# Attention scores as two fp32r parts in two row halves of TensorE, the output turned by block transposes, and the expert tables in three steps

## The chip, the cores and the metric

The kernel runs on one core of one Trainium2 chip. The metric is the device time of one execution in microseconds (us). TensorE is called PE here (its weight loads PEld), VectorE DVE, ScalarE ACT, GpSimd POOL and SyncE SP.

## The reference, cut to what matters

The input is x of 8 batches by 512 tokens by 256 features. After a layer norm come two attention mixers with layer norms between them, and then a mixture of 8 experts of which each token takes 2.

```python
# token mixer: 16 heads of 16 features, the same projection for queries and keys
dot = einsum('bhnd,bhmd->bhnm', qk, qk);  q2 = sum(qk * qk, -1)
logits = (2 * dot - q2[..., :, None] - q2[..., None, :]) / sqrt(dh) * tau
out = einsum('bhnm,bhmd->bhnd', softmax(logits), v) -> (b, n, 256) @ Wo
# channel mixer: 8 heads of 32 channels over the 512 tokens, the same form
# experts: softmax router, top 2, gelu(x @ w1 + b1) @ w2 + b2, weighted sum
x = x + layernorm(attention(layernorm(x)));  x = x + layernorm(ffn(layernorm(x)))
```

All of it is float32. Where the kernel before wants more than bf16 or fp32r gives, it splits a number into parts and multiplies the parts.

## The kernel before, in words

**Order of the work.** Each engine has its own program, and all five are made from one schedule by hand. A batch b is a body of 16 positions (`schedule`, L87). At each position comes the attention of batch b (`att`), then the steps that tables name for that position: POST_AT for batch b-1 (what follows its attention), LATE_AT for b-2 (router), EARLY_AT for b+2 (first norm) and PRE_AT for b+1 (its projections), and then `att_end`. Batches 0 and 1 fill the pipeline, 2 to 5 run in a loop, and 6 and 7 drain it. After batch 7 come the experts: 16 units of 512 rows and 7 of 256, one after the other. What is left of batches 6 and 7 is put between their groups by slots (TAIL_AT, L77); a unit of 512 rows has 16 slots, 8 in its first product and 8 in its second.

**Scores.** At a position PE makes the scores of two units (one head each, 256 keys by 512 queries), four matmuls of 512 columns, into two buffers of PS (L974). ACT turns each unit into E with one exponential of 1024 elements (L589). PE may write the scores of unit u when the exponential of unit u-2 has ended. The operands OPA and OPB hold 102 rows: q in three bf16 parts, paired so that one product gives six terms, and the norms in three parts with ones against them. DVE makes the parts (L696 to L700 for q, L713 to L719 for the norms), SP stores them in memory and loads them in their pairing (L325 to L335 and L371, L377), 11 transfers to a group of four heads. In the first batch ACT's queue loads the keys and norms of the first group.

**The second product.** At `att_end` PE multiplies E by the values (L957): four heads side by side in four column groups of 32, float32 in two passes, eight instructions to a position. ACT copies the sums to OT once in four positions (L597).

**After the attention.** `untok` turns OT with 16 PE transposes (L1036) into PSUM, DVE divides by the sum of the weights (L730, L732) into ON, `ontok` turns ON back with 8 PE transposes (L1047) and ACT copies them to OTN (L549), and `proj` multiplies by Wo (L1058). Then follow the channel mixer's steps: z2, x2t, qkc (L1058), gram (L1093), dist (L1102), soft_c, weights_c, mix (L1111), weff (L1120) and, a body later, chan (L1058 again) with `chan_add`. POOL makes the residual that the projection is added to. The positions 0, 5 and 9 carry chan, proj and qkc, 16 instructions each; at position 12 PE has no step.

**Tables.** DVE works out which rows each expert unit takes. `fill_begun` (L1229), 20 dependent operations, does it for the 5 units that batches 0 to 5 fix; it comes at position 9 of the last body. `fill_tables` (L1281), 51 dependent operations, does the rest at slot 52, and until it ends POOL holds the gather of unit 5. From unit 5 on the second product of the experts is in the joined form (L1767, L1768), before that in the plain one (L1772).

**Start.** SP issues the transfers of x, the vectors, the constants and the weights, with the last four weights in one transfer (L361), and PE's first scores wait for the norms of the first group.

## Time and profile before

| | |
|---|---|
| median of 3 runs | 1119.0 us (1118.0 to 1121.36) |
| the profiled execution's own time | 1118.23 us |
| span of its trace | 1116.4 us |
| mean granted PE clock | 0.975 of 2.4 GHz |
| PE, PEld, DVE, ACT, POOL busy | 92%, 63%, 60%, 65%, 34% |
| first scores; bodies 0, 1, 2 to 5, 6, 7 start at | 32.0; 32.0, 76.4, 136.2, 401.5, 468.0 us |
| last expert unit ends, last output | about 1060 us, 1116 us |

The bodies' starts are the first scores (L974) of position 0 in PE's timeline. A loop body takes 265.3 / 4 = 66.3 us. A busy share is an average over stages; the windows of the trace give it stage by stage.

### The profile page before, as it was taken

Reading aid. Unit: us, or ns where it says so; the run is one execution under the profiler, and the core shown is the slowest. Engines: PE = TensorE matmul, PEld = TensorE weight load, DVE = VectorE, ACT = ScalarE, POOL = GpSimd, SP = SyncE. Lnnn points to the kernel's source line nnn. Section 1 sums busy time; section 2 is a strip of 40 time slices with the busy share of each in tenths; the row PEclk is TensorE's granted clock in tenths of the full one; section 3 lists DMA queues with packets and bytes.
Section 4 is the critical chain, followed back from the end, with each engine's and each line's share of the span. In section 5 each row is a group of like instructions: output and inputs, shape, how many; then the busy total and the mean of one; then the engine's idle time right before and its main releaser. Section 6 shows DMA issues by size and latency. Waiting matters only on the chain. (4 is left out here: it accounts for less than half of the span.)

```text
span 1116.4 us, 17406 instructions
## 1 busy us (share of the span) xinstructions
PE 1032.4 (92%) x5756; PEld 702.8 (63%) x5756; DVE 671.4 (60%) x1902; ACT 721.1 (65%) x1106; POOL 384.5 (34%) x353
## 2 busy tenths in 40 slices
PE   5899999999999999998899996999999999989966
PEld 3234545555455455544588875888888888878842
DVE  5225265454735645354785777677677776679927
ACT  2797767667776766666655662676677766768804
POOL 5121030513323141224426243444433443254315
PEclk9899999999999999999999987999999999989989
DMA  7673816427082542832433133334443344446456
GB/s 267 133 246 61 264 31 204 122 84 256 18 261 73 174 150 69 275 148 91 147 100 115 62 135 123 124 133 148 147 161 119 138 143 142 151 143 224 149 215 256
DMA packets 48960, 167.47 MB, mean 150 GB/s; under 512 B 10160, under 2 KB 16688, under 8 KB 42864
## 3 DMA queue, kind: packets, MB, share of 16 engines
q1 hardware_dynamic: 38170, 136.94, 36.9%
q0 software_dynamic: 10560, 29.14, 8.2%
q8 instruction: 40, 0.66, 0.3%
q10 hardware_dynamic: 150, 0.41, 0.2%
q14 instruction: 40, 0.33, 0.1%
HBM read 102.74 MB, written 63.70 MB: 149 GB/s over the span
## 5 line engine op out<-in xcount | busy, mean ns | idle before, releaser
L589 ACT ACTIVATE E<-PS,VV 128x1024 f32<-128x1024 f32 x256 | 271.6, 1119 | 73.7 <-PE PS L974 72.6
L1737 PE MATMUL PH<-XP,W1P 128*128 128x512 f32 (+1 forms) x1104 | 233.1, 369 | 4.9 <-DVE HP L1678 4.5
L1737 PEld LDWEIGHTS PH<-XP,W1P 128*128 128x128 f32 x1104 | 185.8, 192 | 44.5 <-DVE HP L1678 8.1
L974 PE MATMUL PS<-OPB,OPA 102*128 102x512 bf16 x512 | 137.9, 386 | 11.4 <-DMA OPB<-norm_parts 5.7
L1678 DVE TENSOR_TENSOR HP<-PH,HP 128x512 fp32r<-128x512 f32 x156 | 106.7, 686 | 64.8 <-ACT HP L1584 64.3
L957 PE MATMUL PO<-E,VA 128*32 128x512 f32 x1024 | 143.5, 610 | 0.0
L1579 ACT ACTIVATE PH<-PH,B 128x512 f32<-128x512 f32 (+1 forms) x184 | 107.5, 596 | 53.9 <-PE PH L1737 44.9
L1502 POOL DMA_INDIRECT choice_rows<-Y,DI x78 | 79.3, 1016 | 182.3 <-DVE Y L1635 160.8
L974 PEld LDWEIGHTS PS<-OPB,OPA 102*128 102x128 bf16 x512 | 37.7, 98 | 155.4 <-ACT E L589 68.7
L1570 ACT CAST W2P<-WG 128x512 fp32r<-128x512 f32 x92 | 56.9, 621 | 103.6 <-PE PB L1768 63.6
L462 POOL DMA_INDIRECT expert_rows<-PAY,SLOT x64 | 62.7, 979 | 157.5 <-issue 80.1
L1767 PE MATMUL PY<-W2P,HP 128*128 128x512 f32 x288 | 110.6, 412 | 5.0 <-DVE Y L1635 5.0
L1672 DVE TENSOR_TENSOR W2P<-WG,W2P 128x512 fp32r<-128x512 f32 x92 | 82.0, 900 | 43.5 <-ACT W2P L1570 42.6
L1584 ACT CAST HP<-PH 128x512 fp32r<-128x512 f32 x156 | 91.7, 588 | 4.9
L1495 POOL DMA_INDIRECT XG<-expert_rows,RI x78 | 82.4, 1056 | 32.5 <-issue 26.1
L1768 PE MATMUL PY<-W2P,HP 128*128 128x256 f32 x288 | 81.6, 283 | 0.0
L1767 PEld LDWEIGHTS PY<-W2P,HP 128*128 128x128 f32 x288 | 55.2, 192 | 18.2 <-DVE Y L1635 6.6
L1767 PE MATMUL PB<-W2P,HP 128*128 128x512 f32 x176 | 65.6, 395 | 0.0
L1667 DVE TENSOR_TENSOR W1P<-WG,W1P 128x512 fp32r<-128x512 f32 x92 | 59.6, 687 | 8.3 <-ACT W1P L1563 8.3
L1772 PE MATMUL PY<-W2P,HP 128*128 128x256 f32 x480 | 63.6, 292 | 0.0
L1772 PEld LDWEIGHTS PY<-W2P,HP 128*128 128x128 f32 x480 | 60.8, 198 | 0.1
L1058 PE MATMUL PB<-WB,OTN 128*128 128x256 f32 x256 | 58.8, 383 | 0.2 <-issue 0.2
(254 smaller groups left out, 1611.2 us busy)
## 6 DMA issues: line engine op xcount, KB each, us to landing
expert_rows<-ZERO SPq DMA_DIRECT2D x8, 4160.0 KB, 12.8
WG<-experts SPq DMA_DIRECT2D x23, 1152.0 KB, 5.1
WG<-experts SPq DMA_DIRECT2D x23, 1028.0 KB, 5.2
OPB<-q_parts SPq DMA_DIRECT2D x192, 64.0 KB
YC<-choice_rows SPq DMA_DIRECT2D x8, 1024.0 KB, 13.0
q_parts<-QP SPq DMA_DIRECT2D x48, 128.0 KB
OPA<-q_parts SPq DMA_DIRECT2D x31, 192.0 KB
X<-x SPq DMA_DIRECT2D x8, 512.0 KB, 11.1
```

The source lines that it names most:

```text
L589: a.activation(E[:, s % 2, h, :, :], PS[:, u % 2, :, :], ACT.Exp, scale=vec("tau_t")[:, 4 * (s // 2) + h:4 * (s // 2) + h + 1]).then_inc(e ...
L957: i = t.matmul(PO[32 * h:32 * h + 32, :], VA[:, par, 2 * jp + jc, 4 * g + h, :], E[:, s % 2, h, jc, :], start=(jp == 0 and jc == 0), stop= ...
L974: ins = t.matmul(PS[:, u % 2, jc, :], OPA[0:KA, m, key:key + P], OPB[0:KA, m, hh * N:hh * N + N], start=True, stop=True)
L1495: g.indirect_dma_start(out=XG[:, t % 2, i, :], out_offset=None, in_=rows, in_offset=IND(ap=RI[:, b // HALVES, b % HALVES:b % HALVES + 1], ...
L1579: last = a.activation(r, r, ACT.Gelu_apprx_tanh, bias=B1[:, n * j + k:n * j + k + 1])
L1584: a.copy(region(0, j), PH[:, u % BANKS, :]).then_inc(h_hi, 1)
L1672: v.tensor_tensor(second_piece(1, q), second_raw(q), second_piece(0, q).bitcast(f32), ALU.subtract).then_inc(w2_lo, 1)
L1678: v.tensor_tensor(region(1, j), PH[:, u % BANKS, :], region(0, j).bitcast(f32), ALU.subtract).then_inc(h_lo, 1)
L1737: last = m.matmul(PH[:, u % BANKS, at:at + w], W1P[:, a, k * HID + c * P:k * HID + c * P + P], XP[:, o, k, 0:w], start=(k == 0 and (a, o) ...
L1767: m.matmul(sums(i), HP[:, 0, at:at + P], W2P[:, c, :, :], start=(c == 0), stop=(c == HC - 1), skip_group_check=True)
L1768: last = m.matmul(sums(i)[:, 0, :], HP[:, 1, at:at + P], W2P[:, c, 0, :], start=False, stop=(c == HC - 1), skip_group_check=True)
L1772: last = m.matmul(PY[:, i, :], HP[:, a, at:at + P], W2P[:, c, o, :], start=(c == 0 and (a, o) == terms[0] and i % 2 == 0), stop=(c == HC - ...
```

## The change

Scores: q is split into two fp32r parts (a rounded one and the rest), the norms too, so that three terms of 16 rows and four rows of norms and ones make KA = 52 rows. Two heads lie in partitions 0 to 51 and 64 to 115, and their matmuls write different banks. A unit is now two heads by 128 keys, and ACT makes two exponentials of 512 elements for it. Untok: DVE turns 32 by 32 blocks, divides, and turns the blocks back; the rows of Wo are put in the order that this leaves. Tables: `fill_begun` runs twice, for 5 units and for 2 more (at slot 17), and `fill_tables` does the rest at slot 75. SP alone loads the norms, those of the first group included, and Wo is loaded in 8 transfers.

```diff
-BEGUN = -(-(2 * N * (B - 2) - NE * (2 * SUB - 1)) // (2 * SUB))
+KNOWN = [-(-(2 * N * b - NE * (2 * SUB - 1)) // (2 * SUB)) for b in (B - 2, B - 1)]
+BEGUN = KNOWN[-1]
-KA = 102
-PRE_USES, POST_USES, LATE_USES = 7, 18, 4
+KA = 3 * DH + 4
+PRE_USES, POST_USES, LATE_USES = 7, 12, 4
-LOADS = 16 * 11
-PARTS = 16 * 3
+LOADS = 16 * 12
+PARTS = 16 * 2
-POST_AT = {2: ['residual', 'untok0'], 3: ['untok1'], 4: ['ontok'], 5: ['proj'], 6: ['z2'], 8: ['x2t'], 9: ['qkc'], 10: ['gram'],
-           11: ['dist'], 12: ['soft_c'], 13: ['weights_c'], 14: ['mix'], 15: ['weff']}
+POST_AT = {1: ['untok0'], 2: ['residual', 'untok1'], 4: ['proj'], 5: ['z2'], 7: ['x2t'], 8: ['qkc'], 9: ['gram'],
+           10: ['dist'], 11: ['soft_c'], 12: ['weights_c'], 13: ['mix'], 14: ['weff']}
...
-           17: [('prefix', B - 2)], 18: [('x2t', B - 1)], 20: [('qkc', B - 1)], 22: [('gram', B - 1)], 24: [('dist', B - 1)],
...
-           52: [('tables', B - 1)]}
+           17: [('prefix', B - 2), ('begin', B - 2)], 19: [('x2t', B - 1)], 22: [('qkc', B - 1)], 25: [('gram', B - 1)],
...
+           71: [('prefix', B - 1)], 75: [('tables', B - 1)]}
```

The operands and their loads (`load_queries` is like `load_keys`):

```diff
+        OPA = sb("OPA", [P, KC, PAIRED, N], f32r)
+        OPB = sb("OPB", [P, KC, PAIRED, N], f32r)
...
         def load_keys(eng, b, g):
+            for r in range(2):
+                v = q_rows(g, r)
+                eng.dma_start(operand(OPA, g, r, 0, 2 * DH), v).then_inc(op_loaded[g], 16)
+                eng.dma_start(operand(OPA, g, r, 2 * DH, DH), v[0:DH]).then_inc(op_loaded[g], 16)
...
+        def load_norms(eng, b, g):
+            eng.wait_ge(n_stored, 16 * (b + 1))
+            for r in range(2):
+                eng.dma_start(operand(OPA, g, r, 3 * DH, 2), norm_rows(g, r)).then_inc(op_loaded[g], 16)
+                eng.dma_start(operand(OPB, g, r, 3 * DH + 2, 2), norm_rows(g, r)).then_inc(op_loaded[g], 16)
...
-            sp.dma_start(WB[:, :, :, :], wview[:, 2:6]).then_inc(w_rest, 16)
+            sp.dma_start(WB[:, 1:4, :, :], wview[:, 3:6]).then_inc(w_rest, 16)
+            for h in range(H // KC):
+                q, g = h % 4, h // 4
+                at = 32 * q + DH * g
+                sp.dma_start(WB[at:at + DH, 0, :, :], wview[DH * h:DH * h + DH, 2]).then_inc(w_rest, 16)
```

DVE's split and untok, ACT's exponentials, PE's scores:

```diff
-                    pre.did(v.tensor_tensor(QR[:, m, :], QF[:, m, :], QP[:, m, 0, :], ALU.subtract))
-                    pre.wait()
-                    pre.did(v.tensor_copy(QP[:, m, 1, :], QR[:, m, :]))
-                    pre.wait()
-                    v.tensor_tensor(QP[:, m, 2, :], QR[:, m, :], QP[:, m, 1, :], ALU.subtract).then_inc(qp_ready, 1)
+                    v.tensor_tensor(QP[:, m, 1, :], QF[:, m, :], QP[:, m, 0, :].bitcast(f32), ALU.subtract).then_inc(qp_ready, 1)
...
+                    dve.wait_ge(po_read, GROUPS * b + 2 * m + 2)
+                    for r in range(2):
+                        post.did(v.transpose(TK[:, r, :], OT[:, 2 * m + r, :]))
+                    post.wait()
+                    blocks = TK[:, :, :].rearrange("p r (j e) -> p r j e", e=32)
+                    post.did(v.reciprocal(REC[:, :, :], blocks[:, :, :, DH]))
+                    post.wait()
+                    for r in range(2):
+                        post.did(v.tensor_tensor(TN[:, m, :].rearrange("p (j r d) -> p r j d", r=2, d=DH)[:, r], blocks[:, r, :, 0:DH],
+                                                 REC[:, r, :].unsqueeze(2).to_broadcast([P, N // 32, DH]), ALU.mult))
+                    post.wait()
+                    v.transpose(OTN[:, m, :], TN[:, m, :]).then_inc(otn_ready, 1)
...
+                for jc in range(2):
+                    u = 4 * s + 2 * (pos % 2) + jc
                     act.wait_ge(s_full, UNITS * b + u + 1)
+                    for r in range(2):
+                        h = 2 * (pos % 2) + r
+                        ins = a.activation(E[:, s % 2, h, jc, :], PS[:, u % 2, r, :], ACT.Exp,
+                                           scale=vec("tau_t")[:, 4 * (s // 2) + h:4 * (s // 2) + h + 1])
+                    ins.then_inc(e_ready, 1)
...
+                for jc in range(2):
+                    u = 4 * s + 2 * (pos % 2) + jc
                     at_least(pe, e_ready, UNITS * b + u - 1)
+                    key = (2 * (s % 2) + jc) * P
+                    for r in range(2):
+                        at = HALF_ROWS * r
+                        ins = t.matmul(PS[:, u % 2, r, :], OPA[at:at + KA, m, pair, key:key + P], OPB[at:at + KA, m, pair, :],
                                        start=True, stop=True)
                     ins.then_inc(s_full, 1)
```

PE's untok and ontok and ACT's ontok are taken out; the norms' split loses two of its four operations; and the gather of the first unit of the last table (now unit 7) goes to its ordinary place.

## Rows read from the trace of the kernel before

**Rows 1.** The page, part 1: busy time of the engines.
```profile
PE 1032.4 (92%) x5756; PEld 702.8 (63%) x5756; DVE 671.4 (60%) x1902; ACT 721.1 (65%) x1106; POOL 384.5 (34%) x353
```
**Rows 2.** Busy time by stage: loop bodies, body 7, the tail's first units.
```profile
core 0: us, PE busy (x) PEld busy (x) DVE busy (x) ACT busy (x) POOL busy (x), PEclk, DMA share, GB/s
...
136.20:401.50 265.30, 256.51 (x1493) 137.19 (x1490) 140.35 (x528) 185.44 (x236) 74.21 (x70) 1.00 0.44 140
...
468.00:532.40 64.40, 58.68 (x340) 29.46 (x336) 29.65 (x125) 42.34 (x53) 22.61 (x24) 0.95 0.39 135
532.40:714.00 181.60, 160.38 (x972) 140.58 (x969) 131.59 (x373) 100.15 (x170) 76.92 (x70) 0.93 0.34 115
```
**Rows 3.** PE's timeline in a loop body: start us, length us, line, operation.
```profile
302.54 1.04 PE L974 MATMUL PS<-OPB,OPA 102*128 102x512 bf16 x4
303.41 1.04 PE L1077 MATMUL PB<-KT,ON 128*128 128x128 f32 x8
304.28 0.60 PE L1135 MATMUL PA<-KT,PAY 128*128 128x128 f32 x4
304.81 1.07 PE L957 MATMUL PO<-E,VA 128*32 128x512 f32 x8
305.81 1.04 PE L974 MATMUL PS<-OPB,OPA 102*128 102x512 bf16 x4
306.74 3.69 PE L1058 MATMUL PB<-WB,OTN 128*128 128x256 f32 x16
```
**Rows 4.** ACT's timeline in a loop body.
```profile
348.07 0.59 ACT L528 COPY QF<-PA 128x512 f32<-128x512 f32 x1 [1.16 <-PE PA L1005]
348.56 0.59 ACT L529 CAST QP<-PA 128x512 bf16<-128x512 f32 x1
349.40 2.12 ACT L589 ACTIVATE E<-PS,VV 128x1024 f32<-128x1024 f32 x2 [0.26 <-PE PS L974]
```
**Rows 5.** PE's timeline in the experts: fp32r matmuls of 512 columns.
```profile
714.54 11.36 PE L1737 MATMUL PH<-XP,W1P 128*128 128x512 f32 x48
```
**Rows 6.** The page, part 5: weight loads of those matmuls.
```profile
L1737 PEld LDWEIGHTS PH<-XP,W1P 128*128 128x128 f32 x1104 | 185.8, 192 | 44.5 <-DVE HP L1678 8.1
```
**Rows 7.** DVE's timeline in a loop body: untok, and the split of q.
```profile
350.56 0.42 DVE L732 TENSOR_TENSOR ON<-PB,REC 128x256 f32<-128x256 f32 x1
...
354.07 0.68 DVE L696 TENSOR_TENSOR QR<-QF,QP 128x512 f32<-128x512 f32 x1
```
**Rows 8.** PE's timeline at the start: the first scores.
```profile
32.00 1.89 PE L974 MATMUL PS<-OPB,OPA 102*128 102x512 bf16 x4 [5.73 <-DMA OPB<-norm_parts]
```
**Rows 9.** PE's timeline in the tail: idle before an instruction in brackets.
```profile
552.39 1.19 PE L1036 MATMUL PB<-KT,OT 128*128 128x128 f32 x8 [2.70 <-DVE ON L732]
...
678.55 1.11 PE L1748 MATMUL PT<-KT,XG 128*128 128x128 f32 x4 [8.02 <-DVE XP L1661]
679.32 8.19 PE L1772 MATMUL PY<-W2P,HP 128*128 128x256 f32 x48
...
726.10 0.47 PE L1767 MATMUL PY<-W2P,HP 128*128 128x512 f32 x1
...
731.73 0.60 PE L1748 MATMUL PT<-KT,XG 128*128 128x128 f32 x4
```
**Rows 10.** The same timeline: an undisturbed second product in the plain form.
```profile
708.71 6.00 PE L1772 MATMUL PY<-W2P,HP 128*128 128x256 f32 x48
```
**Rows 11.** DVE's timeline: first and last operation of fill_begun (20) and fill_tables (51), and a wait.
```profile
511.56 0.21 DVE L1253 TENSOR_TENSOR QR<-COUNT,KT 128x56 f32<-128x56 f32 x1
...
516.02 0.07 DVE L1276 MEMSET DUMP<- 128x20 f32 x1
...
661.80 0.15 DVE L1305 SCALAR_TENSOR_TENSOR OT<-TAKEN,COUNT 128x8 f32<-128x8 f32 x1
...
675.70 0.17 DVE L1367 CAST WI<-OT 128x7 int32<-128x7 f32 x1
...
688.85 0.16 DVE L1648 TENSOR_TENSOR NT<-XG 128x4 f32<-128x4 f32 x1 [6.04 <-DMA choice_rows<-Y,DI]
```

More of the change, by code:

```diff
@@ L329, in load_queries, with operand @@
[L329 to L335 removed]
+        def operand(tile, g, r, at, n):
+            first = g % 2 * 2
+            return tile[HALF_ROWS * r + at:HALF_ROWS * r + at + n, g // 2, first:first + 2, :].bitcast(f32)
@@ L545, in scalar_program @@
             do["v0"], do["v1"] = vv(0), vv(1)
-            def ontok(b, par):
-                for m in range(KC):
-                    a.copy(OTN[:, m, :], takep(b, 4 + m)).then_inc(post_free[m], 1)
-            do["ontok"] = ontok
             def x2t(b, par):
                 for k in range(KC):
-                    affine(X2T[:, k, :], takep(b, 8 + k), vec("ln2_w")[:, k:k + 1], vec("ln2_b")[:, k:k + 1]
+                    affine(X2T[:, k, :], takep(b, 2 + k), vec("ln2_w")[:, k:k + 1], vec("ln2_b")[:, k:k + 1]
                            ).then_inc(post_free[k], 1)
@@ L1248, in fill_begun @@
     rows_of, most = COUNT[:, 0, :], STEPS_E // 2 - 1
-    over, full, start, ends = take(NE, most), take(NE), take(NE), take(NE)
+    over, full, start, ends, ahead = take(NE, most), take(NE), take(NE), take(NE), take(NE)
     cube, held = take(NE, NE), take(U, NE)
@@ L1258, in fill_begun @@
     link(v.tensor_tensor(ends, start, full, ALU.add))
-    link(v.tensor_scalar(start, start, -1.0, float(U), ALU.mult, ALU.add))
-    link(v.tensor_tensor(start, start, full, ALU.min))
-    link(v.tensor_scalar(TAKEN[:, :], start, 0.0, None, ALU.max))
     unit = const("unit")[:, 0:2 * U].rearrange("p (u two) -> p u two", two=2)[:, :, 0]
@@ L1928, in constants @@
     put("expert_steps", np.diff(v % NE, prepend=0))
-    put("unit", s // 2)
+    put("unit", np.arange(max(LEFT, 2 * BEGUN)) // 2)
     put("offset", s % 2 * SUB)
```

245 lines of the change are left out of this document (109 added, 136 removed).

## The prediction

> **What bounds the kernel now.** I read the busy shares first: PE has 92%, the next engines 65% and 60% [rows 1]. The windows then tell where. In the loop bodies PE is busy 256.5 of 265.3 us at the full 2.4 GHz, ACT 185 and DVE 140 [rows 2]: PE sets the 66.3 us of a body, and what is taken from PE there comes off the time until ACT is next. Body 7 (64.4 us, 58.7 busy) and the tail with the first expert units (181.6 us, 160.4 busy, clock 0.93) have gaps. Each position is a chain too: ACT needs 2.02 us for its two units, 1.01 for each (2.12 is the length of two that overlap a little) [rows 4]. A position cannot be shorter than that, whatever PE saves.
>
> I checked this reading by adding up a body. On PE four scores take 0.87 us, from their start to the next instruction's; the second product takes 1.00; a 128 column instruction takes 0.109 (eight in 0.87), a 256 column one 0.22 (sixteen in some 3.5) [rows 3]. Between the four transposes at 304.28 (0.44) and the second product at 304.81 there are 0.09 more, which I take as the price of changing the form of the array; I use 0.12. A position is the longer of 1.99 + its steps on PE, and 2.02 + its copies on ACT. From 0 to 15 this gives 5.95, 3.2, 4.6, 4.6, 2.9, 5.5, 3.7, 2.5, 3.9, 7.3, 3.75, 2.9, 2.6, 2.5, 4.6, 5.5: 66.0, against 66.3 measured. So the model may carry the change.
>
> **Scores.** 64 bf16 matmuls of 512 columns in a body become 64 of fp32r with 52 rows, in 32 pairs whose halves may run together. No row shows row halves. Bounds: fp32r at 512 columns takes 11.36 / 48 = 0.237 us in the full array, loads included [rows 5]. If the halves run together, two pairs take 0.47; if not, four take 0.95, against 0.87 now. The nearest row is the second product: eight instructions of 512 columns in four column groups take 1.00 us [rows 3], where eight of 0.237 in a row would take 1.9. The array does run groups side by side, and the two halves write different banks, so I take 0.47: 0.40 less at a position. Then scores and steps no longer have the same form: one more change, between nothing and 0.15; I take the 0.12, at the 13 positions with steps.
>
> The Trainium skill, TensorEngine Tiling (Array Packing), Key Properties, says that changing the tiling mode drains TensorE. The 0.09 above agrees; were each drain a full 0.15, a body would be 0.4 us longer than I say.
>
> **Untok and ontok.** 24 transposes leave PE: 24 x 0.109 = 2.6 us in a body, with them two copies on ACT (1.0 us). In their place DVE has six block transposes of 512 elements, two reciprocals and four products. No row shows a block transpose. The nearest are a subtraction of 512 from SBUF, 0.68 long and 0.6 apart, and the division of 256, 0.42 [rows 7]; I take 0.6 for each transpose, at most 1.2 if it runs at half pace. A half of untok then is 1.2 + 0.3 + 0.7 + 0.7 = 2.9 us, 5.8 in a body in place of some 2.6. The split drops two of its three operations on each half of q and two of four on the norms; with 0.4 for a copy to bf16 (an estimate from the 0.42) and 0.7 for a subtraction that is 3.3 us back. DVE stays near 35 of 61 us: covered, if its order holds. At position 1 untok0 now stands before chan_add, so chan_add ends near 12.7 us into the body, the residual on POOL near 16.6, and untok1 near 15.6. PE's proj at position 4 wants it at 16.2. That is 0.6 us of slack; at half pace PE would wait some 2 us.
>
> **ACT.** 64 exponentials of 512 in place of 32 of 1024. Two copies of 512 stand 0.49 apart, two units of 1024 1.01 [rows 4]: two of 512 cost 0.98, so no more. Bound: 0.6 each, were nothing overlapped, 6 us of a body that has 20 us of ACT to spare, felt only where ACT leads.
>
> **The body after.** With 0.47 + 0.12 + 0.12 + 1.00 = 1.71 plus steps, or ACT's sum: 5.7, 3.2, 3.4, 3.4, 5.2, 2.5, 3.4, 3.9, 5.7, 5.3, 2.6, 2.6, 2.1, 3.1, 5.3, 3.5 = 60.9. That is 5.1 us less than the same sum before. PE's own saving is larger, 6.4 in scores less 1.6 in changes plus 2.6 = 7.4; the rest is lost at positions 1, 5, 7, 11, 12 and 13, where ACT leads. The steps after proj keep their distances: I followed proj's last add, norm, z2 and x2t, and gram, dist, soft_c and mix, and found the waits of before (under 1 us each) moved and not grown.
>
> Four loop bodies give 20.5 us, body 6 some 5, bodies 1 and 7, which miss some steps and have ACT ahead more often, 4.5 each. In body 7 fill_begun moves behind gram's copies, so its 4.5 us [rows 11] keep soft_c instead of dist waiting: even. Body 0 is mostly ACT's: 1.5. Together 36.
>
> **Transfers.** q's parts in memory are 8 bytes for 6, the operands as many bytes as before (96 rows of 2 against 48 of 4, twice), 12 issues for 11 on SP. In the loop PE is idle 3% of the time in all and DMA busy 44% [rows 2], so no load is late now, and I add nothing. At the start PE waits 5.73 us for the norms [rows 8]. The two dropped split operations come before that store, and one queue issues four small loads where two queues issued one each; Wo's eight transfers only delay x of later batches by some 3 us. The gain is between 0 and the 5.73; I take 1, since the keys on ACT's queue still start behind the same copy.
>
> **Tail.** Off: the 2.6 us of transposes of batch 7, the idle 2.70 at 552 [rows 9], about 2.5 us of small waits by wider slots, and POOL's held gather, which made DVE wait 6.04 for a send [rows 11] and PE about 1.8. On: the second fill_begun, 26 operations at 4.5 / 20 = 0.23 each, 5.9 us of DVE at slot 17, of which PE's three banks hide a part: 4.5. fill_tables runs 14.0 us and leaves PE idle 8.02, then slow: 8.19 against 6.00 [rows 9, 10, 11]. With 25 subtiles for 29 it takes 13.4; at slot 75 PE has four chunks (6 us) less DVE's lag before it: idle 9.7, 1 us worse. Units 5 and 6 keep the plain form: a half costs 714.54 - 708.71 = 5.83 for the joined one's 731.73 - 726.10 = 5.63, so 0.4 a unit, 0.8 for two [rows 5, 9, 10]. Sum: -9.6 + 6.3 = -3.
>
> **The sum.** -36 - 1 - 3 = -40 against the profiled execution's own 1118.2, thus 1078.2. That execution stands 0.8 us below the median, so for a median **1079 us**. Unknown sizes: pair time 0.47 to 0.6 (+0 to +10), changes of form 0 to 0.15 (-10 to +3), untok at half pace (0 to +13), tail (-6 to +6). Alone this case spans 1066 to 1098.
>
> **Rival 1: the halves do not run together.** For it: no row shows them. Against it: the column groups do. Scores then take 0.95; with the change of form a position costs 0.2 more, 13 x 0.2 = 2.6, which is what the transposes gave. Bodies stay at 66, start and tail give 4: 1115.
>
> **Rival 2, slower: weight loads in the open.** An fp32r load is 192 ns long [rows 6]. Were the halves to run one after the other, with one load exposed before each unit, the scores would take 0.95 + 0.38 = 1.33: +0.46, +0.12 for the change, 13 x 0.58 - 2.6 = +4.9 in a body, 32 over the kernel, less 4: 1147. It is slower as soon as the four scores take over 0.95. Against it: 48 such loads hide behind their matmuls in 11.36 us, no more than 20 ns each showing [rows 5].
>
> The Trainium skill, TensorE: Matmul & The Clock Gate, Part 3, says that a load overlaps running matmuls only if it goes to other row groups. Here each second pair reloads the same halves. The 11.36 us contradicts this in the full array, where all loads use the same rows; in halves no run shows it yet.
>
> **Rival 3: PE becomes faster, but DVE's chain is late.** Block transposes at 1.2, proj late by 2 to 3 us, and everything after it behind: +2.5 x 6 bodies and some in the tail: 1096. For it: only 0.6 us of slack. Against it: SBUF operations of that size take 0.6.
>
> **How the numbers follow.** My case 0.70, rival 3 0.12, rival 1 0.11, rival 2 0.07. A measurement can tell 0.3%, 3.4 us, from no change: rival 1 lies at that border, 0.05 of it within, 0.01 above, 0.05 below. Faster 0.87, same 0.05, slower 0.08. The range of 8 in 10 takes my case nearly whole and rival 3: 1064 to 1100.
>
> **What would show it.** Right: the scores start two and two, the two pairs of a position within about 0.47; loop bodies of 61 us; ACT's exponentials 0.5 apart; PE's idle time put down to ACT at positions 1, 5, 7, 11 to 13; the tables' idle near 10 us in unit 4. Wrong: each score starting 0.2 us after the last (rival 1); gaps before loads (rival 2); PE waiting for OTN at position 4 with DVE's transposes over 1 us (rival 3); or a granted clock below 1.00 in the loop, which I do not expect, with PE over 90% busy.

## The result, and the profile after

The changed kernel took 1135.05 us (median of 4 runs, 1130.59 to 1135.85), the kernel before, beside it on the same chip, 1118.5. The ratio is 1.0129, 95% interval 1.0097 to 1.0161: **slower by some 14 us**, where I had forecast 1079. The profiled execution took 1130.59 us (span 1128.8), that of the kernel before 1118.23 (span 1116.4): 12.4 us between them.

The table cuts both traces at the same marks: the first scores, ACT's copies of OT (the first of each body), the first expert product, PE's transposes ahead of unit 5's second product, the first product of the last unit, and PE's first instruction of stage 3. The marks do not fall on the borders of bodies, so a forecast stands beside the stretch that lies nearest.

```
stretch                                before    after   difference   forecast
to the first scores                     32.0      31.95     0.0         -1
first scores to first OT copy           18.0      20.5     +2.5         -1.5 (body 0)
to OT of body 2                        113.0     111.7     -1.3         -4.5 (body 1)
to OT of body 6 (four bodies)          265.2     259.6     -5.6        -20.5
to OT of body 7                         67.2      68.2     +1.0         -5
to the first expert product             42.7      44.6     +1.9         -4.5 (body 7)
to unit 5's second product (tail)      187.7     193.7     +6.0         -3
to the last unit's first product       327.0     327.3     +0.3          0
to stage 3's first PE instruction       20.4      27.9     +7.5          0
to the end                              43.2      43.4     +0.2          0
```
By the first scores of each body, body 0 takes 48.2 us for 44.4, body 1 57.6 for 59.8, a loop body 65.0 for 66.3, body 6 64.5 for 66.5, and body 7, up to the first expert product, 74.2 for 70.1. Between the forecast of -40 and the +12.4 of the traces lie 52 us: 34.5 in the bodies, 9 in the tail, 7.5 in the gap before stage 3 and 1 at the start. (The last expert unit of the kernel before ends at 1065.1 us, not at about 1060 as its table says.)

The page of the changed kernel: busy time of the engines, ACT's exponentials, PE's scores.
```profile
PE 999.9 (89%) x5628; PEld 685.7 (61%) x5628; DVE 685.9 (61%) x1904; ACT 745.6 (66%) x1346; POOL 385.8 (34%) x353
...
L607 ACT ACTIVATE E<-PS,VV 128x512 f32<-128x512 f32 x512 | 310.8, 716 | 67.9 <-PE PS L993 67.3
...
L993 PE MATMUL PS<-OPB,OPA 52*128 52x512 f32 x512 | 108.3, 474 | 33.1 <-ACT E L607 26.2
```
PE works 32 us less than before [rows 1], and the kernel is longer. ACT works 25 us more: the exponentials bring 39 (310.8 here, 271.6 on the page of before), and ontok's 16 copies are gone.

Busy time by stage: four loop bodies, body 7, and the tail with its first units.
```profile
core 0: us, PE busy (x) PEld busy (x) DVE busy (x) ACT busy (x) POOL busy (x), PEclk, DMA share, GB/s
137.67:397.83 260.16, 238.07 (x1396) 125.15 (x1393) 149.47 (x520) 198.24 (x356) 75.05 (x70) 1.00 0.52 148
462.32:531.50 69.18, 55.37 (x317) 28.58 (x313) 34.80 (x130) 46.27 (x84) 23.52 (x24) 0.90 0.41 135
531.50:714.50 183.00, 155.57 (x948) 134.12 (x948) 137.12 (x390) 98.50 (x168) 74.63 (x68) 0.95 0.33 112
```
Against [rows 2]: a loop body is 65.0 us for 66.3. PE's work in it fell by 4.6 us (256.5 to 238.1 over four), its idle time rose from 2.2 to 5.5. So 3.3 of the 4.6 us that left PE came back as waiting.

PE's timeline in a loop body, positions with scores, the wait at proj, and scores that ACT holds up.
```profile
307.07 0.73 PE L993 MATMUL PS<-OPB,OPA 52*128 52x512 f32 x4
307.73 2.05 PE L1090 MATMUL PB<-ON 128*128 128x128 f32 x16
...
317.01 0.50 PE L993 MATMUL PS<-OPB,OPA 52*128 52x512 f32 x2
318.17 0.49 PE L993 MATMUL PS<-OPB,OPA 52*128 52x512 f32 x2 [0.66 <-ACT E L607]
...
351.78 3.72 PE L1056 MATMUL PB<-WB,OTN 128*128 128x256 f32 x16 [2.12 <-DVE OTN L750]
```
Four scores take 0.66 us to the next instruction where nothing waits, for 0.87 in [rows 3]. My sum had 0.59 for this: 0.47, and 0.12 for the change of form behind the scores. Taken apart, the operations on PS of one position (ns: shortest, median, longest):
```profile
L993 PEld LDWEIGHTS PS<-OPB,OPA x4: 182/184/186, 301.2 to 301.3; 52*128 52x128 f32 x4
```
```profile
L993 PE MATMUL PS<-OPB,OPA x4: 393/444/496, 301.2 to 301.5; 52*128 52x512 f32 x4
```
The four matmuls start within 0.34 us and are each 0.39 to 0.50 long: the halves do run together. The 0.19 by which the step is longer than 0.47 is the length of one of its loads. That the first load of a position lies in the open is my reading; no run here isolates it. The Trainium skill, TensorE: Matmul & The Clock Gate, Part 3, has loads overlap running matmuls only for other row groups. The trace does not agree for the second pair: its two loads start at 301.27 and end at 301.46, while the matmuls of the first pair, in the same halves, are recorded from 301.17 to 301.66. At the first load of a step the numbers allow the rule.

ACT's timeline in the loop body: four exponentials are 2.47 us long for the 2.12 of two long ones [rows 4].
```profile
302.24 2.47 ACT L607 ACTIVATE E<-PS,VV 128x512 f32<-128x512 f32 x4
```
Back to back they stand 0.57 apart, so two of 512 cost 1.14, where one of 1024 cost 1.01. Body 0, which is mostly ACT's, grew by 3.8 us (e2 below, the scores alone, has the same 48.2).

DVE's timeline in a loop body: both halves of untok (block transposes, then the two products), chan_add between them; then POOL's residual.
```profile
340.14 1.31 DVE L741 STREAM_TRANSPOSE Z3T<-OT 128x512 f32<-128x512 f32 x2
...
341.87 0.76 DVE L747 TENSOR_TENSOR ON<-Z3T,REC 128x256 f32<-128x256 f32 x2
...
344.79 1.23 DVE L842 TENSOR_TENSOR X<-X 128x1024 f32 x1 [0.16 <-DVE X L840]
345.94 1.30 DVE L741 STREAM_TRANSPOSE Z3T<-OT 128x512 f32<-128x512 f32 x2
...
347.65 3.24 DVE L747 TENSOR_TENSOR ON<-Z3T,REC 128x256 f32<-128x256 f32 x2
350.93 0.71 DVE L750 STREAM_TRANSPOSE OTN<-ON 128x512 f32<-128x512 f32 x1
```
```profile
346.69 1.90 POOL L472 TENSOR_TENSOR X<-X,SM 128x1024 f32<-128x1024 f32 x1 [0.19 <-POOL SM L470]
348.67 1.95 POOL L475 TENSOR_TENSOR X<-X,SM 128x1024 f32<-128x1024 f32 x1
```
A block transpose takes 0.65, near the 0.6 I had taken. But the same two products take 0.76 in the first half and 3.24 in the second, where POOL's residual runs from 346.7 to 350.6. Taken apart, the first product takes 1.21 us and ends 0.28 after POOL's first operation, the second takes 2.11 and ends 0.28 after POOL's second. The surplus of 2.5 us covers the 2.12 for which PE waits at proj.

The kernel before holds the control. POOL's residual ran beside untok's products there too, and did not slow them:
```profile
349.20 1.89 POOL L453 TENSOR_TENSOR X<-X,SM 128x1024 f32<-128x1024 f32 x1
```
The product at 350.56 in [rows 7] lies inside this operation and took 0.42. It read one operand from PSUM; the new products read both from SBUF. None of the products of L732 that meet the residual in that trace is longer than 0.43, and the new block transpose that meets it (the second at 345.94) takes 0.67.

At the start nothing moved: 31.95 for the 32.00 of [rows 8]. The tail, PE: idle before an instruction in brackets (compare [rows 9]).
```profile
555.57 2.93 PE L1745 MATMUL PH<-XP,W1P 128*128 128x512 f32 x6 [3.74 <-DVE HP L1686]
...
594.72 1.65 PE L1745 MATMUL PH<-XP,W1P 128*128 128x512 f32 x3 [5.85 <-DVE HP L1686]
...
716.46 13.95 PE L1745 MATMUL PH<-XP,W1P 128*128 128x512 f32 x48 [10.47 <-DVE XP L1669]
730.25 0.60 PE L1756 MATMUL PT<-KT,XG 128*128 128x128 f32 x4
```
The second fill_begun runs on DVE from 588.35 to 593.84 (26 operations, 5.5 us), and holds HP. The 48 products behind the tables' wait take 13.95 where undisturbed ones take 11.36 [rows 5]: the granted clock is 0.50 from 708.3 us on, for 13.7 us.

The end of the experts' block: POOL's last instruction there (ns), and PE's first of stage 3.
```profile
L1161 POOLq DRAIN  x1: 9221/9221/9221, 1075.9 to 1075.9; - x1
```
```profile
1085.45 4.82 PE L1853 MATMUL S<-KT 128*128 128x128 f32 x21 [15.58 <-PEq L1161]
```
In the kernel before, this drain took 1707 ns and PE was idle for 8.08 us. Nothing in the program touches that place.

### The profile page after: what moved, and what is told of

Its sections match the earlier page's. It is cut to its first block and busy times, and to the rows that moved or that the text cites. A ratio compares the mean times of both kernels' runs of the same rounds, so it can differ in the third digit from the quotient of the medians.

```text
span 1128.8 us, 17345 instructions
## 1 busy us (share of the span) xinstructions
PE 999.9 (89%) x5628; PEld 685.7 (61%) x5628; DVE 685.9 (61%) x1904; ACT 745.6 (66%) x1346; POOL 385.8 (34%) x353
## 5 line engine op out<-in xcount | busy, mean ns | idle before, releaser
L607 ACT ACTIVATE E<-PS,VV 128x512 f32<-128x512 f32 x512 | 310.8, 716 | 67.9 <-PE PS L993 67.3
L1587 ACT ACTIVATE PH<-PH,B 128x512 f32<-128x512 f32 (+1 forms) x184 | 107.6, 596 | 64.8 <-PE PH L1745 55.5
L1686 DVE TENSOR_TENSOR HP<-PH,HP 128x512 fp32r<-128x512 f32 x156 | 107.0, 687 | 67.8 <-ACT HP L1592 67.3
L993 PEld LDWEIGHTS PS<-OPB,OPA 52*128 52x128 f32 x512 | 42.8, 187 | 156.7 <-ACT E L607 107.8
L993 PE MATMUL PS<-OPB,OPA 52*128 52x512 f32 x512 | 108.3, 474 | 33.1 <-ACT E L607 26.2
L1775 PE MATMUL PY<-W2P,HP 128*128 128x512 f32 x256 | 99.0, 416 | 5.3 <-DVE Y L1643 5.3
L1780 PE MATMUL PY<-W2P,HP 128*128 128x256 f32 x672 | 85.7, 285 | 0.0
L1780 PEld LDWEIGHTS PY<-W2P,HP 128*128 128x128 f32 x672 | 81.9, 191 | 0.1
L1056 PE MATMUL PB<-WB,OTN 128*128 128x256 f32 x256 | 63.4, 404 | 17.4 <-DVE OTN L750 15.2
L1776 PE MATMUL PY<-W2P,HP 128*128 128x256 f32 x256 | 72.9, 285 | 0.0
L1056 PEld LDWEIGHTS PB<-WB,OTN 128*128 128x128 f32 x256 | 50.3, 202 | 30.6 <-issue 13.2
L1525 POOL TENSOR_TENSOR BW<-WG,G 128x1024 f32<-128x1024 f32 (+1 forms) x23 | 41.3, 1796 | 58.3 <-DVE DI L1665 58.3
## 6 DMA issues: line engine op xcount, KB each, us to landing
YC<-choice_rows SPq DMA_DIRECT2D x8, 1024.0 KB, 12.7
```

What stands on the lines that cost most here:

```text
L607: ins = a.activation(E[:, s % 2, h, jc, :], PS[:, u % 2, r, :], ACT.Exp, scale=vec("tau_t")[:, 4 * (s // 2) + h:4 * (s // 2) + h + 1])
L993: ins = t.matmul(PS[:, u % 2, r, :], OPA[at:at + KA, m, pair, key:key + P], OPB[at:at + KA, m, pair, :], start=True, stop=True)
L1056: ins = t.matmul(ps[:, c * D:c * D + D], lhs[:, k, cc * P:cc * P + P], rhs(k), start=(k == 0), stop=(k == KC - 1))
L1587: last = a.activation(r, r, ACT.Gelu_apprx_tanh, bias=B1[:, n * j + k:n * j + k + 1])
L1686: v.tensor_tensor(region(1, j), PH[:, u % BANKS, :], region(0, j).bitcast(f32), ALU.subtract).then_inc(h_lo, 1)
L1775: m.matmul(sums(i), HP[:, 0, at:at + P], W2P[:, c, :, :], start=(c == 0), stop=(c == HC - 1), skip_group_check=True)
```

## The experiments

Kernels that ran together shared a chip and the runs of the kernel before. Its median was 1121.0 beside e1 to e4, 1130.0 beside e5 to e8, 1132.6 beside e9 to e12, 1118.5 beside e13 to e16, and 1119.2 beside e17 and e18. So ratios are compared, not times. The second and third of these groups ran on one chip, on which everything took 1% longer.

```
                                           ratio to before, 95%
e1  the changed kernel                     1.0119  1.0061-1.0177
e2  before + scores                        1.0086  1.0059-1.0112
e3  before + block transposes              1.0045  1.0018-1.0072
e4  before + tables in three steps         1.0106  1.0074-1.0139
e5  before + scores + blocks               1.0135  1.0078-1.0191
e6  changed, proj one later                1.0334  1.0281-1.0387
e7  before + tables, old slots             1.0040  1.0008-1.0072
e8  before + one wait on POOL              1.0025  0.9993-1.0058
e9  changed, chan_add behind untok1        1.0329  1.0277-1.0381
e10 e5, chan_add behind untok1             1.0069  1.0040-1.0099
e11 e10, exponentials of 1024              0.9962  0.9933-0.9992
e12 e3, chan_add behind untok1             1.0036  1.0003-1.0068
e13 e3, whole chain of steps later         0.9895  0.9861-0.9930
e14 e5, whole chain of steps later         1.0003  0.9965-1.0042
e15 e7, tables at slot 75                  1.0066  1.0039-1.0092
e16 changed, norms by two queues           1.0157  1.0113-1.0201
e17 e15, prefix at slot 71                 1.0065  1.0040-1.0090
e18 e13 again                              0.9897  0.9869-0.9924
```

**e1, the changed kernel again.** No edit.

> The changed kernel itself, so that its stages can be compared with those of the parts below under the same conditions. All theories: 1130 to 1136 us. Against the kernel before, the profiled execution of the changed one stood so: body 0 +3.7, bodies 1 to 6 -9.4, body 7 +4.1, tail to expert unit 6 +6.4, the stretch between the last expert product and the third stage's first PE instruction +7.5. If the last is a property of the program, the gap before PE's first instruction of stage 3 is 15 to 16 us again; if it is chance, it is 8 as in the kernel before and the profiled time falls to 1123.

The gap before stage 3 was 15.58 again, so it belongs to the program. The loop differed: three of four bodies took 66.5 to 66.7 us, at a mean granted clock of 0.97 where the first trace had 65.0 at 1.00. Busy time and clock around the wait for OTN (columns as in the windows above; the clock is the third from the end):
```profile
287.00:289.00 2.00, 0.56 (x1) 0.50 (x2) 1.28 (x2) 1.45 (x3) 2.00 (x3) 0.73 0.00 0
289.00:291.00 2.00, 2.00 (x6) 1.59 (x5) 0.00 (x0) 0.00 (x0) 0.46 (x1) 0.50 0.00 0
291.00:293.00 2.00, 2.00 (x10) 1.70 (x10) 0.69 (x1) 0.00 (x0) 0.00 (x0) 0.91 0.00 0
```
PE had waited 2.23 us for OTN until 288.44; from then its clock was at 1.2 GHz (0.50) for some 3 us, a dip that costs 1.6 us, in three bodies. The loop's first wait, 2.25 us at 156.7, had none beside it, nor had any of the same waits in the first trace. What the wait costs is thus not fixed: 2.1 us, or 3.7 with the dip.

**e2, e3, e4, the three parts alone.** Each takes its own lines of the diff onto the kernel before.
```
e2: scores by row halves, splits, exponentials of 512, norms by one queue
e3: untok by block transposes, Wo permuted, proj at position 4
e4: KNOWN, second begin, wide slots of the tail, no held gather
```

> The kernel before with the score part alone (fp32r parts, row halves, norms). Theory A (the scores' form is what ate the gain: exponentials of 512 at 0.57 in place of 0.505 per 512, and q's path at the start): loop body 66 to 67 us, body 0 +3.7, time 1120 to 1128. Theory B (the scores are a gain, DVE's block transposes lose it): loop body 63 to 64 us, time 1105 to 1110.

> The kernel before with the block transposes alone. Theory A: the 24 transposes of 0.109 that leave PE give 2.6 us in each of seven bodies less the waits for OTN that the changed kernel showed (2.2 a body), loop body 64 to 65, time 1108 to 1114. Theory B: PE waits for OTN longer than the transposes took, loop body 66.5 or more, time 1120 to 1130.

> The kernel before with the tables in three steps and the wider tail slots alone. As I forecast: start and loop as before, tail 3 us shorter, 1115. Theory C (the tail's +6.4 and the gap of +7.5 before stage 3 belong to this part): 1125 to 1132, with bodies as before, the stall for HP at the second begin, and the gap of 15 us before stage 3. If the gap belongs to another part: 1121 to 1125.

Every part alone makes the kernel slower: theory A for the scores, but worse than it said (loop bodies 67.8, median 1130.9), theory B for the blocks (66.1 to 68.0, with 8.2 us of waits for OTN in four bodies), theory C for the tables (loop bodies 66.3 as before; stalls of 5.84 and 10.03; gap 15.59; median 1135.5, above its range). In e2 and e3 the clock in the loop fell to 0.97 and 0.98, in e4 it stayed at 1.00. In e2 no wait for OTN exists: four of its five dips come behind a wait of 0.65 for E and one of 0.4 to 0.5 for OH. The tables' part by itself is nearly as slow as the whole change (1.0106 against 1.0119 beside it), so scores and blocks together seemed to give about nothing there, while their sum would be +1.3%.

**e5 to e8.** e5 leaves the tables' part out; e6, e7 and e8 are these edits:
```diff
e6
-POST_AT = {..., 4: ['proj'], 5: ['z2'], 7: ['x2t'], 8: ['qkc'], ...
+POST_AT = {..., 5: ['proj'], 6: ['z2'], 8: ['x2t'], 9: ['qkc'], ...
e7: on e4, TAIL_AT of before, with
+           17: [('prefix', B - 2), ('begin', B - 2)], ... 50: [('prefix', B - 1)], 52: [('tables', B - 1)]}
e8: on the kernel before
+            if t == 4:
+                pool.wait_ge(begun["begun_ready"], 1)
```

> The changed kernel without the tables' part: one fill_begun, slots, held gather and joined units of before, with the new scores and the block transposes. If the parts only add up (scores +9.9, blocks +6.5, tables +14.6 alone): 1137. Theory A (the first two repair one another, since both spend PE time that the other leaves free, and the loop is 65.1 us at full clock or 66.6 where the clock dips once a body; the tables' part costs 14): loop body 65 to 66.7, gap before stage 3 8 us, time 1118 to 1122.

> The changed kernel with proj at position 5, z2 at 6, x2t at 8 and the rest one later too, as the kernel before had them; nothing else is touched. Theory A (PE's wait of 2 us for OTN and the clock of 1.2 GHz that follows it, which took 4 x 1.6 us in the second look at the changed kernel, are what the loop lost): no wait for OTN, clock 1.00 in the loop, loop body 62 to 63.5, time 1110 to 1120. Rival (ACT's longer exponentials set the body, and a wait removed at one position comes back at the next): loop body still 65, time 1128 to 1133.

> The kernel before with the tables in three steps, and the slots of before (prefix at 50, tables at 52, the chain of waits of before between them). Against the tables' part as it was (1135.5): if the second begin at slot 17 costs the tail (stall for HP near 597, then the slow clock), that stall is here too. If the stall of 10 us at the tables is from their place at slot 75, it is gone or hidden here, since unit 5 is known before: 5 to 9 us faster. If the gap of 15.6 us before stage 3 comes from the late last sends of expert rows, it is 8.1 here; if from POOL's instructions, one wait more than before, it stays 15.6. In all 1118 to 1122 with the gap gone, 1125 to 1130 with it.

> The kernel before with one more wait on POOL, for a semaphore that has long been raised (begun_ready, ahead of the gather of unit 4). It can hold nothing up. If the length or place of POOL's instructions makes the drain at the end of the block 9.2 us in place of 1.7, the gap before stage 3 is 15.6 us here and the time 1126 to 1128. If it is from the order of POOL's transfers, the gap stays 8.1 and the time 1118 to 1121.

e5 was slower than I expected: its ratio, 1.0135, is the plain sum of e2's and e3's (1.0131), so the two parts did not repair one another here. Three of its loop bodies took 68 us, each with the wait for OTN, longest 3.5 us. The gap was 8.08. In e6 the loop's wait for OTN was gone (0.3 us in four bodies) and bodies took 64.1 to 66.9, better than e5's beside it; but waits for NF grew from 1.4 to 6.4 us, and body 7, which has z3t0 at position 4, ahead of proj, waited for its input:
```profile
491.30 1.11 PE L1132 MATMUL PA<-KT,PAY 128*128 128x128 f32 x4 [9.46 <-DVE PAY L854]
```
The stretch to OT of body 7 thus took 74.9 us, 68.6 in e5. The rest of its 3.3% came in the tail, with the tables' part. While POOL issued 16 indirect transfers one behind the other, PE was idle several times with nothing to wait for:
```profile
726.63 0.37 PE L1780 MATMUL PY<-W2P,HP 128*128 128x256 f32 x1 [2.01 <-issue]
```
These waits came to 9.9 us in all, to 7.0 in e9 on the same chip, and to none in e1 or e4 on another. Why this chip does so stays open. e7 has the gap at 8.09 and costs 0.4%, where I had expected none; e8, with as many waits on POOL, has 8.09 too, and its time can't be told from that of the kernel before. So neither the second begin nor POOL's instructions make the gap: the wide slots do. They make the stall at the second begin too: it stands at slot 17 in e7 as well, and there PE waits 1.0 us behind it, not 5.8 (1.0 for HP in e15 and e17). The old slots have x2t right behind it, the wide ones leave that slot empty.

**e9 to e12, the collision, and the size of the exponentials.**
```diff
e9 (on the changed kernel), e10 (on e5), e12 (on e3)
-LATE_AT = {0: ['chan'], 1: ['chan_add'], 4: ...
+LATE_AT = {0: ['chan'], 2: ['chan_add'], 4: ...
-LAST_AT = {0: ['chan'], 1: ['chan_add'], 2: ['chan_stats'], ...
+LAST_AT = {0: ['chan'], 2: ['chan_add', 'chan_stats'], ...
e11, on e10
-                    for r in range(2):
-                        h = 2 * (pos % 2) + r
-                        ins = a.activation(E[:, s % 2, h, jc, :], PS[:, u % 2, r, :], ACT.Exp,
+                    h = 2 * (pos % 2)
+                    ins = a.activation(E[:, s % 2, h:h + 2, jc, :], PS[:, u % 2, :, :], ACT.Exp,
```

> The changed kernel with chan_add on DVE put behind untok1 (position 2 for 1), so that POOL's residual, which waits for chan_add, no longer starts while DVE multiplies by the reciprocals. In the changed kernel the second half's two products took 3.24 us with POOL's two subtractions and products of 1024 beside them, the first half's 0.76. Theory P (the two engines share their way to memory; that is the 2.2 us for which PE waits for OTN): both halves take 0.76, no wait for OTN, loop body 62.5 to 63.5 with the clock at 1.00, ratio to the changed kernel 0.985. Rival (DVE is late for want of time, and the wait moves to the residual and proj's add): body 65 to 66.7 as before, and PE waits for proj's banks or z2 instead.

> The same order without the tables' part (scores and block transposes on the kernel before). Theory P: as the last in the loop, gap before stage 3 back at 8.1, tail as in the kernel before: 14 us less than the last, that is 0.985 to 0.995 of the kernel before. Rival: 1.01 of it.

> The kernel of the last, with one exponential of 1024 elements for the two heads of a unit, with the scale of the first head for both: 32 in a body for 64. The second head of each pair thus gets the wrong temperature. If the splitting of the exponentials costs what it took on ACT (0.57 for 512 against 0.505 for half of 1024, 4.5 us of ACT a body, and the waits of 2.5 us a body for E), body 60 to 61 us, as I had forecast for the change, and 12 to 18 us less in all. If ACT is not what bounds, under 3 us less.

> The kernel before with the block transposes and the order of the last three, without the new scores. Theory P: 24 transposes leave PE (2.6 us a body) and no wait for OTN comes in their place: loop body 63.7 to 64.5, time 0.98 to 0.99 of the kernel before, so better than both kernels. If the first experiment's loss of the blocks was not the collision: body 66 to 68, 1.005.

The products of untok (ns: shortest, median, longest), first in four loop bodies of the changed kernel, then in four and a half of e9:
```profile
L747 DVE TENSOR_TENSOR ON<-Z3T,REC x16: 418/817/2110, 146.8 to 348.8; 128x256 f32<-128x256 f32 x16
```
```profile
L747 DVE TENSOR_TENSOR ON<-Z3T,REC x18: 416/422/427, 150.5 to 415.1; 128x256 f32<-128x256 f32 x18
```
With POOL's residual behind them none is longer than 0.43 us: the collision is shown, and PE no longer waits for OTN. PE's waits in e9's loop (us in total, times, longest):
```profile
PE PS L993 <- ACT E L607: 12.9, 26, 0.7
PE PA L1132 <- DVE NF L722: 3.2, 4, 0.8
PE PB L1074 <- DVE ON L783: 2.0, 4, 0.8
```
Yet three of four bodies take 65.2 to 65.7, no less than the 65.0 of the changed kernel at full clock, and the fourth takes 68.6. The 8.2 us turned into more waits for E (10.0 before the edit), for NF (1.4) and for ON (0). So the mechanism was theory P's and the outcome the rival's; what the edit saved is mainly dips, since three bodies of e5 on this chip were 68. Not all of them: the body of 68.6 has one with no wait longer than 0.65 us, for E, before it:
```profile
188.00:190.40 2.40, 1.49 (x10) 0.27 (x10) 1.61 (x11) 2.40 (x6) 0.00 (x0) 0.99 1.04 411
190.40:200.60 10.20, 10.19 (x31) 6.30 (x32) 2.04 (x12) 5.86 (x10) 2.73 (x3) 0.50 0.64 251
```
In all, e9 is as slow as e6, from the same tail.

e10, without that tail, came out at 1.0069 for e5's 1.0135: the order is worth 0.7%, yet the kernel stays slower than the one before, as the rival had it. In its body 7 the wait for OTN was gone as well, and PE waited 5.2 us for z3t0's input instead.

e11 tells the price of the split; it leaves out the scale of each pair's second head, so it is a measurement and no version to use. Against e10 beside it: 1127.3 to 1138.7, 11.4 us or 1.0%. Bodies 0, 1 and 2 of the traces took 46.0, 55.5 and 63.3 us for 47.8, 57.5 and 65.4, about 2 us a body, not the 4.5 that I had put at the top; over the four loop bodies it is 2.2 us in all (261.4 for 263.7), as dips and the waits for ON came elsewhere. ON's waits grew again, to 7.1 us in the loop. No body took the 60 to 61 in which I had believed.

e12 did not beat the kernel before (1.0036): PE waited 2.05 us a body for ON at x2t, since the residual, proj's add and z2 all came later. Position 7 was too early for x2t.

**e13, e14, e18: the whole chain one later.**
```diff
on e3 (e13, e18) and on e5 (e14)
+LATE_AT = {0: ['chan'], 2: ['chan_add'], 4: ['chan_stats'], 5: ['chan_norm'], 8: ['z3t0'], 9: ['z3t1'], 10: ['logits'], ...
+POST_AT = {1: ['untok0'], 2: ['residual', 'untok1'], 5: ['proj'], 6: ['z2'], 8: ['x2t'], 9: ['qkc'], 10: ['gram'], ...
+POST_LAST = {...}    # the changed kernel's POST_AT, used in body 7
```

> The kernel before with the block transposes, chan_add behind untok1, and proj, z2, x2t and what follows one position later in the loop (z3t0 to prefix one later too), with the order of the changed kernel kept in body 7. Theory P (24 transposes less on PE are worth 2.6 us a body once nothing else waits: the last version waited 2.0 us a body for ON at x2t and 0.8 for NF, each wait followed by a slower clock): body 63 to 64 at clock 1.00, ratio 0.985 to 0.992, better than both kernels. Rival (the chain through DVE and ACT around proj is as long as the body allows, so a wait removed comes back at another step): body 65 to 67, ratio 1.00.

> The same order with the new scores too. If the pairs of scores are a gain of 0.5 us a body on PE and the split exponentials the loss of up to 4.5 on ACT, this is 2 to 8 us slower than the last (body 64 to 65, body 0 3.5 us longer), ratio 0.99 to 1.00. If the scores are worth what I forecast: 20 us faster than the last.

> The version of e13 once more, in five rounds, since it is the one that beats both kernels and chips have differed by 1% in the kernel before: ratio 0.985 to 0.993 again if what it gains is PE's work and no accident of one chip; above 0.997 if the gain was the chip's.

Four loop bodies of e18, and PE's waits in them:
```profile
133.20:385.70 252.50, 246.48 (x1396) 126.14 (x1392) 162.62 (x544) 180.21 (x228) 75.42 (x69) 1.00 0.45 147
```
```profile
PE PS L982 <- ACT E L591: 4.2, 15, 0.4
PE PA L1032 <- DVE PX L892: 1.3, 4, 0.3
```
Bodies of 63.1, clock 1.00, 1.5 us of waits in each. **The block transposes with the new order are worth 3.2 us a body:** e13 and e18, on two chips, are 1.0% faster than the kernel before (1107.7 us in the last). They are the best versions found, faster than both kernels. PE's work is 2.5 of the 3.2 (246.5 us in four bodies for 256.5), which is the transposes. The other 0.7 is idle time, and seems to be the order's: the waits for NF, 3.3 us in the loop before and 3.2 in e3, are gone with z3t0 one later. The order without the transposes was not run.

e14 adds the new scores: undisturbed bodies of 63.7 to 63.9. PE is busy 59.6 us of them for e18's 61.6, but waits 3.2 for E for 1.05, and its body 0 is longer by 4 us. In this kernel, with two exponentials for each unit, the scores are no gain at all. Part of the 1.1% may be chance: in the traced execution the first scores came at 35.5 us, not near 32, and the last loop body, with a dip behind waits of 0.65, took 66.9; the nine runs spread from 1112 to 1136.

**e15 and e17, where the gap comes from; e16, the norms.**
```diff
e15, on e7
-           52: [('tables', B - 1)]}
+           75: [('tables', B - 1)]}
e17, on e15
-           50: [('prefix', B - 1)],
+           71: [('prefix', B - 1)],
e16, on the changed kernel: load_norms takes keys and queries apart
-                    load_norms(sp, b, 0)
+                    load_norms(sp, b, 0, keys=False)
+                        load_norms(act, b, 0, queries=False)    # behind load_keys(act, b, 0)
```

> The kernel with the tables in three steps in the slots of before (gap before stage 3 of 8.1), with one step moved: tables from slot 52 to 75, while the last sends of the experts' rows stay behind the prefix at slot 50. If the gap of 15.6 us (POOL's drain of 9.2 in place of 1.7) comes with late sends of rows, it stays at 8.1; if it comes with the late tables or the place of the gather behind them, it is 15.6. The tail: PE waits about 10 us in unit 4 for the tables, and the time is 5 us longer without the gap.

> The kernel of e15 (tables in three steps, tables at slot 75) with one more step moved: the prefix of batch 7, and with it the last eight sends of the experts' rows, from slot 50 to 71. The rest of the tail's chain stays in the slots of before. If the gap of 15.6 us before stage 3 (POOL's drain of 9.2 us in place of 1.7) comes with the late sends, it is back: 15.6, and the time 7 to 8 us above e15's. If it needs the whole chain of wide slots, it stays 8.1.

> The changed kernel with the norms of the first group loaded as before: those of the keys by ACT's queue, those of the queries by SP's. In the changed kernel all four came by SP, and the first scores started at 31.95 to 32.3 as in the kernel before (32.0). If one queue was as good as two: first scores at 31.5 to 32.5. If two are better once the loads are halves: 30 to 31. The block end's gap stays 15.6.

POOL's drain at the end of the block, in e15 and in e17:
```profile
L1167 POOLq DRAIN  x1: 1707/1707/1707, 1079.3 to 1079.3; - x1
```
```profile
L1167 POOLq DRAIN  x1: 9221/9221/9221, 1073.3 to 1073.3; - x1
```
The one step between them is the prefix of batch 7, with the last eight sends of rows behind it. Sent at slot 71, the block ends 7.5 us later (PE idle 15.61), over 300 us after the sends. The drain took one of two lengths in all 20 traces: 9221 ns in the seven with the prefix at 71, 1707 ns in the thirteen with it at 50. How a send so far back lengthens it is open. The whole times of e15 and e17 do not differ, since e17's last expert product came 6 us earlier (1054.9 for 1060.9): e15 had also waited 6.22 us for HP at 688.9, e17 had not. So the gap is shown by the drain, not by the ratio.

e16's first scores came at 35.72, behind the norms of the keys. But with one queue they came at 31.8 to 33.2 in seven traces and at 35.1 and 35.5 in two (e11, e14). The run can't tell, and what one queue is worth stays open between 0 and 3.7 us.

## Why the prediction was wrong

**The step that failed is the body after, 60.9 us.** It measured 65.0. Three of its terms were off. Put into the same sum they give some 65.4 (an estimate): 0.7 at the ten positions where PE leads, 1.6 at the six where ACT leads, and 2.2 of waiting for OTN. The last, an overlap that I had not priced, is the largest. Each by itself is no measure of what its removal gives: e9, without the wait for OTN, had bodies no shorter at full clock, as E, NF and ON then held PE.

First, the step of the scores, "I take 0.47" and 0.12 for one more change of form: 0.66 measured for the 0.59, 0.07 a position. The halves do run together, so rival 1 fell. Ahead of the scores a change of form adds nothing: they start 1.00 us after the second product before and after.

Second, "two of 512 cost 0.98, so no more": 1.14. It made ACT's two units of a position 2.29 long for 2.02, and PE waited 2.5 us a body for E, in 20 short waits of up to 0.7 over four bodies. I had bounded the price at 6 us of ACT a body "felt only where ACT leads"; by e11 it is about 2 us a body where no dip falls in. The row I used, two copies, overlapped more than exponentials do.

Third, "A half of untok then is 2.9 us": the first half took 3.2, the second 5.7. My 0.6 a transpose was right (0.65). I had priced the two products from a row whose product read one operand from PSUM, and POOL's residual beside it did not slow it; with both operands in SBUF it does. I had worked out myself that the residual would run from some 12.7 to 16.6 us into the body, across untok1, without asking what the two do to each other. In place of the 0.6 us of slack proj waited 2.1 us for OTN. The Trainium skill has this rule, and I did not draw on it: SBUF — State Buffer, section SBUF: two separate sides, says that VectorE with two inputs from SBUF and GpSimd reading SBUF share one pair of ports as an exclusive lock, so that the later one stands still for the other's whole instruction. The trace agrees: in the changed kernel both products of untok1 end 0.28 us after the operation of POOL that was running when they were due, and in the kernel before the product with one operand in PSUM was not held. **Rival 3 thus named the right wait at the right place, for the wrong reason**, and its 1096 was too low, as it kept the other two terms.

Right were: PE's saving by the transposes (2.5 us a body in e13 and e18, 2.6 by my count); ACT leading at late positions; full clock in the first trace's loop. "Or a granted clock below 1.00 in the loop, which I do not expect" failed from the second trace on: waits of some 2 us for OTN could have 3 us at 1.2 GHz beside them, and in e2, e9 and e14 waits of 0.65 us for E did.

**Body 7** was to give 4.5 us and lost 4.1. PE waited 4.63 us for OTN there (the two products took 3.03 for 0.76, so by length the collision is half of it), and the 16 instructions of proj behind it took 6.45 us for 3.7. No version mended this body. e13 and e18 kept the changed kernel's order in it: their stretch to OT of body 7 is 68.1 and 68.3. Where chan_add was moved there too, e10, the wait went to z3t0's input (5.2 us).

**Body 0** was to give 1.5 us and lost 3.8, all of it with the scores (48.2 in e2, 44.4 in e3). Long exponentials gave back 1.8 of it (e11); the other 2 us are open.

**The tail** was to give 3 us and lost 6.0. The second fill_begun was priced at 4.5 and cost 5.85, though by e7 only together with the wide slots; the tables' wait at 9.7 and was 10.47. Missing was the untok of batch 7, now on DVE between expert products (HP 3.74 us late, in every kernel with block transposes). The slow clock is not new: behind the tables it cost 2.6 us for the 2.2 of before, and over the whole tail it was low for 27 us in place of 24. What I took off, "2.5 us of small waits by wider slots", hardly showed: the waits under 2.6 us add up to 8.0 for 8.5. In all PE waited 28.0 us for 19.2.

**The gap before stage 3**, 7.5 us, I did not have, nor could the trace of before show it. With it and the tail the tables' part is a loss by itself (e4). That is more than half of the 12.4 us between the two traces.

**The Trainium skill's drain at a change of form** (TensorEngine Tiling (Array Packing), Key Properties) can't be read off here on its own: 0.66 less 0.47 holds whatever of a load and of such a drain shows, and no run parts them. In the kernel before, the scores are followed after 0.87 us by a step in the same form and after 0.97 by the second product, which agrees with the 0.09 of the prediction.

The chance of 0.08 for slower was too small in one way above all: four edits, each with a wait or a collision that could turn it, were summed at the value of each one's best case.

## What to carry to other kernels

When work moves from the busiest engine to another, price the moved operation beside what will run then: an operation with both operands in SBUF may take four or five times as long beside GpSimd, while the same operation with one of them in PSUM does not suffer, and a wait of 2 us on TensorE may cost nearly twice its length with the low clock that comes with it. Moving it is half of the change; the steps behind it have to be moved as a chain, since with one step moved the wait comes back at the next (OTN, then E, NF and ON), and with all of them moved it was gone. And time a change in its parts: here one of three was worth 1% once its order was mended, and the other two hid it.

## What the runs showed of the hardware

- GpSimd holds VectorE up where VectorE reads two operands from SBUF: two products of 256 elements (128 partitions) took 0.76 us alone and 3.24 beside GpSimd's two operations of 1024, each ending 0.28 us after GpSimd's. GpSimd was hardly slower (1.90 and 1.95 us, for 1.89 and 1.89 in the kernel before). With one operand in PSUM the product beside them took 0.42, as without them.
- ScalarE, exponentials from PSUM, start to start: 512 elements 0.57 us, 1024 elements 1.01.
- fp32r matmuls of 52 rows in the two row halves run together: four of 512 columns in 0.66 us to the next instruction, for 0.87 of four bf16 ones of 102 rows.
- A 128x512 block transpose on VectorE takes 0.65 us in a pair, 0.71 alone.
- TensorE's granted clock fell to 1.2 GHz beside three of four waits of 2.1 to 2.25 us in the loop of one execution (e1) and not in another of the same program, and in e9 for 10.2 us behind a wait of 0.65.
- GpSimd's drain at a block's end took 1.707 or 9.221 us, by when the last indirect transfers of another tensor had been issued, over 300 us before (20 traces; the cause is open).
- On one chip (e6, e9) TensorE stood still for up to 2 us at a time, with no wait that the profile shows, while GpSimd issued 16 indirect transfers in a row.
